# Query rows by three bfloat16 products, routing weights and the last experts' weights loaded in earlier stages

## The chip, the cores and the metric

One core of one Trainium2 chip (trn2). The metric is the device time of the whole program in microseconds; lower is better.

## The reference

A two-layer graph network on 3125 nodes of 256 features and 100,000 edges. Layer 0 is an edge aggregation, a linear attention and an eight-expert layer. Layer 1, on which the change bears, is

```
q, k, v = xn @ Wq + bq, xn @ Wk + bk, xn @ Wv + bv            # 8 heads of 32
scores  = einsum(q[dst], k[src] + ep) * scale * edge_weight    # per edge and head
attn    = segment_softmax(scores, dst)
gnn     = segment_sum(attn * v[src], dst) @ Wo + bo            # then its feed-forward
mix     = linear attention, LayerNorm, relu feed-forward, LayerNorm
x       = xn + gnn + mix
logits  = mean(x) @ Wr + br                                    # one routing for all nodes
top_i, top_w = the two largest of softmax(softmax(logits) * scale)
out     = x + LayerNorm(sum_j top_w[j] * expert[top_i[j]](x) + x)
```

All of it is float32, and the row `q[dst]` of every edge must come out exactly to float32 accuracy, since the softmax follows.

## The kernel before

The program is a row of stages, each a block in which every engine has a queue of its own; a stage ends when all engines are through. Nodes are kept as `NT` = 25 tiles of 128 rows. Edges are sorted by destination and cut into 832 chunks of 128 that each belong to one node tile; 16 chunks make a *window*, and there are `NW` = 52 windows.

`stage_mid` makes q, k and v, spills what later stages need, and runs the linear attention. Its second part works through 14 blocks (`lines`, `NB` = 14) of 128 features by up to 512 nodes: TensorE multiplies (L2372), ScalarE adds the bias (`line`, L2557), VectorE takes the negative part (`below`, L2718), ScalarE exponentiates it (`exp`, L2563), VectorE joins the two (`feature`, L2724), TensorE adds the block into a divisor (L2379). Then come the division (L2772, L2774), the products, a LayerNorm and `rows` (L2792, L2794), which leaves the residual row of the mix branch in `sh.work`; ScalarE's `keep_back` and SyncE's stores of `xt_d` (L2293) end the stage.

`stage_flash` is the edge attention, with the mix branch's feed-forward laid in between. Key and value rows are gathered by GpSimd (`gather`, L2989) into a ring of two windows. The body of one window asks for the rows of window s and closes window a = s - 1. For each quarter g of a window (4 chunks) ScalarE makes a one-hot matrix `mem_t` (`place`, L3126 and L3129), TensorE multiplies it by the q rows of the node tile (`ask`, L3021: 4 products of 128 x 128 by 128 x 256) into the single PSUM tile `query`, and VectorE multiplies the gathered keys by it (`mult`, L3226). Since there is one `query`, `ask(g + 1)` waits for `mult(g)`, and `mult` waits for `ask`. VectorE's order in a body is hand-written: `add(0)`, `within`, `across`, `add(1)`, `lower`, `mult(0)`, `rescale`, `weigh(0)`, `weigh(1)`, `mult(1)`, `add(2)`, `weigh(2)`, two `reduce`, `mult(2)`, `weigh(3)`, `add(3)`, `reduce(2)`, `mult(3)`, `reduce(3)`, `scale`. TensorE's is: transpose of the scores, `up` of the feed-forward (L3058), ends (L3065), `ask(0)`, carried (L3071), `down` (L3077), two small products (L3082, L3083), `ask(1)`, `collect` (L3034) and `fold` (L3041) 0 to 2, `ask(2)`, fold 3, collects 4 and 5, fold 4, `ask(3)`, the rest. A tile whose number is read at run time costs a register instruction ahead of its first product (ISA in the rows of the order).

The q product is float32 and shows as two records (a weight load and a matmul each) per product of the program. SyncE's queue in this stage is, per window: goal (L2948), eight edge loads (L2954), eight flag loads (L2960), steps; and per two windows one tile of the feed-forward's input. VectorE adds the feed-forward's result to `sh.work` in place (L3331). At the end of the stage SyncE waits for the last window but one, loads `xn` back (L2976), and GpSimd adds a bias to it (L3002).

`stage_route` loads the three routing arrays (L3580 to L3582), forms the logits (L3589) and writes the two expert numbers (L3642). `stage_ffx` reads the numbers on SyncE ahead of each of its loads (L2041 to L2043), waits for all three arrays of expert 0 and runs up (L2064) and down (L2073) of both experts, output last.

## Time and profile before

| what | us |
|---|---|
| median of 3 runs (3642.55 to 3644.26) | 3642.98 |
| the profiled execution, its own time | 3640.97 |
| its span, first to last instruction | 3639.0 |
| TensorE busy | 3021.7 |
| VectorE busy | 2119.2 |
| ScalarE busy | 1716.8 |
| GpSimd busy | 1923.4 |

The stages follow each other in the span: edges and aggregation to about 1210, the first experts to about 1550, `stage_mid` to 1853, `stage_flash` from there to 3188, its output projection and feed-forward to 3430, routing to 3443, the last experts to the end. Instruction times are in ns where the rows say so, all others in us; "idle before" is the time for which the engine had nothing to do just before an instruction, with what released it.

### The profile page before, as it was taken

The numbers are of one execution on the slowest core, as the hardware profiler recorded it, in microseconds if no ns is written. First come the engines' busy times: TensorE is split into PE (matmuls) and PEld (weight loads), VectorE is DVE, ScalarE is ACT, GpSimd is POOL, SyncE is SP. The second block draws the span as 40 slices with busy tenths as digits, with TensorE's granted clock in tenths as the row PEclk, the third lists the DMA queues.
The fourth block names the chain that finished last, engine by engine and source line by source line (L and its number), as shares of the span: only waits on it lengthen the run. The fifth ranks groups of instructions, "written<-read, shape, count | busy, mean of one in ns | idle before, by whom it ended". The sixth has DMA issues, their size and how long they took to land. (4 is left out here: it accounts for less than half of the span.)

```text
span 3639.0 us, 50484 instructions
## 1 busy us (share of the span) xinstructions
PE 3021.7 (83%) x12620; PEld 2281.7 (63%) x12620; DVE 2119.2 (58%) x4741; ACT 1716.8 (47%) x3980; POOL 1923.4 (53%) x1876
## 2 busy tenths in 40 slices
PE   2778677778778599779849999999999999889798
PEld 2556555555555588656437777777777777656565
DVE  6333334333334500175559999999999999843415
ACT  2434333333333322233246666667666666542323
POOL 3777777777773344301036666666666666530010
PEclk9777767887868599989769999999999999889899
DMA  6555555555551256641057777777777777510001
GB/s 162 147 146 149 140 156 140 156 141 147 143 146 34 68 197 219 185 160 59 9 182 221 219 215 223 210 219 221 218 216 222 218 214 224 154 67 0 27 0 36
DMA packets 354070, 547.21 MB, mean 150 GB/s; under 512 B 172814, under 2 KB 224275, under 8 KB 353509
## 3 DMA queue, kind: packets, MB, share of 16 engines
q0 software_dynamic: 113216, 348.74, 33.1%
q1 hardware_dynamic: 232710, 183.43, 17.0%
q10 hardware_dynamic: 7887, 12.08, 1.0%
q8 instruction: 104, 1.70, 0.2%
q14 instruction: 153, 1.25, 0.1%
HBM read 493.34 MB, written 51.90 MB: 150 GB/s over the span
## 5 line engine op out<-in xcount | busy, mean ns | idle before, releaser
L2989 POOL DMA_INDIRECT store<-kv_d,src_of x832 | 869.5, 1045 | 422.5 <-issue 245.7
L859 POOL DMA_INDIRECT agg_rows<-xn_d,src_of x832 | 791.5, 951 | 268.4 <-issue 243.1
L1031 PE MATMUL agg_sums<-agg_rows,agg_member 128*128 128x257 f32 x1664 | 582.8, 497 | 255.2 <-DVE acc L923 132.8
L872 ACT ACTIVATE agg_rows<-agg_rows,weight_of 128x256 f32<-128x256 f32 x832 | 375.2, 500 | 614.6 <-DMA agg_rows<-xn_d,src_of 611.7
L1031 PEld LDWEIGHTS agg_sums<-agg_rows,agg_member 128*128 128x128 f32 x1664 | 374.4, 245 | 415.2 <-DVE acc L923 185.2
L923 DVE TENSOR_TENSOR acc<-acc,agg_sums 128x257 f32 x416 | 176.3, 424 | 580.6 <-PE agg_sums L1031 566.1
L3021 PE MATMUL flash_query<-q,flash_mem_t 128*128 x1664 | 412.7, 392 | 50.6 <-DVE store L3226 38.8
L3034 PE MATMUL flash_sums<-store,flash_member 128*128 128x264 f32 x1664 | 424.8, 388 | 2.2 <-DVE store L3291 2.2
L3021 PEld LDWEIGHTS flash_query<-q,flash_mem_t 128*128 128x128 f32 x1664 | 312.7, 193 | 103.7 <-issue 57.4
L3034 PEld LDWEIGHTS flash_sums<-store,flash_member 128*128 128x128 f32 x1664 | 318.4, 191 | 56.8 <-issue 2.2
L3144 ACT ACTIVATE acc<-flash_sums 128x264 f32 x416 | 159.2, 383 | 254.5 <-PE flash_sums L3041 254.5
L3226 DVE TENSOR_TENSOR store<-store,flash_query 128x1024 f32<-128x1024 f32 x208 | 252.3, 1213 | 39.8 <-PE flash_query L3021 39.7
L3041 PE MATMUL flash_sums<-acc,ident 128*128 x832 | 269.5, 406 | 1.9 <-ACT acc L3144 1.5
L3135 ACT ACTIVATE flash_member<-lane,lane_of 128x128 f32<-128x128 f32 x832 | 264.1, 395 | 0.0
L3219 DVE TENSOR_TENSOR store<-store,flash_ep 128x1024 f32<-128x1024 f32 x208 | 252.5, 1215 | 14.8 <-DMA flash_ep<-ep_d 13.5
L3291 DVE TENSOR_TENSOR store<-store,flash_pa 128x1056 f32<-128x1056 f32 x208 | 258.4, 1264 | 0.0
L3230 DVE TENSOR_REDUCE flash_dots<-store 128x32 f32<-128x1024 f32 x208 | 247.8, 1212 | 1.8
L3041 PEld LDWEIGHTS flash_sums<-acc,ident 128*128 128x128 f32 x832 | 145.9, 190 | 64.2 <-issue 48.3
L914 DVE TENSOR_SCALAR agg_member<-lane,lane_of 128x128 f32<-128x128 f32 x832 | 178.9, 304 | 9.5 <-issue 0.4
L1021 PEld LDWEIGHTS agg_edge<-agg_we,agg_feats 128*128 128x128 f32 x832 | 146.8, 249 | 31.4 <-issue 10.5
L1815 DVE TENSOR_TENSOR moe_y<-moe_down,moe_b 128x512 f32<-128x512 f32 x32 | 22.1, 691 | 244.1 <-PE moe_down L1653 244.1
L3126 ACT ACTIVATE flash_mem_t<-flash_goal,minus_row 128x512 f32<-128x512 bf16 x208 | 148.0, 712 | 22.0 <-PE flash_query L3021 15.3
(483 smaller groups left out, 4597.6 us busy)
## 6 DMA issues: line engine op xcount, KB each, us to landing
moe_w<-in_L_ffn_W_dram SPq DMA_DIRECT2D x64, 512.0 KB, 4.5
agg_feats<-in_ef_t_dram SPq DMA_DIRECT2D x208, 128.0 KB
flash_goal<-goal_d SPq DMA_DIRECT2D x52, 512.0 KB, 4.3
agg_rows<-xn_d,src_of POOLq DMA_INDIRECT x832, 2.8
ep_d<-agg_ep SPq DMA_DIRECT2D x52, 256.0 KB
store<-kv_d,src_of POOLq DMA_INDIRECT x832, 4.1
flash_ep<-ep_d SPq DMA_DIRECT2D x416, 32.0 KB
flash_flags<-flags_d SPq DMA_DIRECT2D x416, 32.0 KB
```

Source lines behind the costliest of these rows:

```text
L859: pool.indirect_dma_start(rows[:, q, 0:D], None, sh.xn_d, bass.IndirectOffsetOnAxis(ap=sh.src_of[:, c:c + 1], axis=0)).then_inc(gathered[u ...
L872: act.activation(rows[:, q, 0:D], rows[:, q, 0:D], ACT.Copy, scale=sh.weight_of[:, bass.ds((UI * i + u) * SUBS + k, 1)]).then_inc(weighted, 1)
L1031: last = pe.matmul(sums[:, j % 4, 0:W], member[:, c % (2 * BI * SUBS), :], rows[:, c % NB, :], start=(c % SUBS == 0), stop=(c % SUBS == SU ...
L2989: pool.indirect_dma_start(ring[:, s, :], None, sh.kv_d, bass.IndirectOffsetOnAxis(ap=sh.src_of[:, c:c + 1], axis=0)).then_inc(gathered[p][ ...
L3021: last = pe.matmul(query[:, c * D:(c + 1) * D], mem_t[:, g % 2, c * P:(c + 1) * P], sh.q[:, bass.ds(t, 1), :], start=True, stop=True)
L3034: pe.matmul(sums[:, n % 3, 0:W], member[:, g % 2, c, :], ring[:, a.side * WS + 4 * g + c, HI_], start=(k == 0), stop=False)
L3041: pe.matmul(sums[:, n % 3, 0:W], sh.ident[:, :], sh.acc[:, bass.ds(tiles[n], 1), :, :].rearrange("p a h v -> p (a h v)"), start=False, sto ...
L3135: act.activation(member[:, g % 2, k, :], sh.lane[:, :], ACT.Abs, scale=-1.0, bias=sh.lane_of[:, bass.ds(WS * a.at + (4 * g + k), 1)])
L3219: dve.tensor_tensor(r, r, ep[:, s.side, 4 * g:4 * g + 4, :].unsqueeze(2).to_broadcast([P, 4, H, DH]), ALU.add).then_inc(add_done, 1)
L3226: dve.tensor_tensor(r, r, query[:, :].rearrange("p (k f) -> p k f", k=4), ALU.mult).then_inc(mult_done, 1)
L3230: dve.tensor_reduce(dots[:, g * 4 * H:(g + 1) * 4 * H].rearrange("p (k h) -> p k h", h=H), key_rows(s, g).rearrange("p k (h d) -> p k h d" ...
L3291: dve.tensor_tensor(r, r, e.unsqueeze(3).to_broadcast([P, 4, H, VW]), ALU.mult).then_inc(pv_ready, 1)
```

## The change

The q rows are split exactly into three bfloat16 parts: the upper half of each float32 word (read in place, every second bfloat16 of `sh.q`), the rounded rest, and what is left (`sh.q_low`, in the memory of `stage_mid`'s qkv weights). High and middle part overwrite `sh.q`. `ask` makes three bfloat16 products per chunk where it made one float32 product, all into the same PSUM columns; `mem_t` is bfloat16. The splitting is added to `stage_mid`'s second part: `rest` and `lowest` on VectorE, `parts` on ScalarE, seven pieces of up to four tiles.

To make room, `sh.work` goes to DRAM: five stores in `stage_mid`, one load and one store of a tile per two windows in `stage_flash`, the whole back at its end. Its memory holds the feed-forward's second weights, hidden rows and input. The routing arrays are loaded in the output projection's stage. The last experts' weights are loaded from within `stage_route`, as soon as the expert numbers are written; `stage_ffx` waits for the first weights and bias (32), and for the second weights apart.

```diff
@@ stage_mid, SyncE
+                    sp.wait_ge(rows_done, e)
+                    sp.dma_start(sh.work_d[:, a:e, :], sh.work[:, a:e, :]).then_inc(sh.work_out[n], 16)
@@ stage_mid, ScalarE
+                def parts(n):
+                    a, e = SPLIT[n]
+                    act.wait_ge(rest_ready, n + 1)
+                    act.activation(sh.q_parts[:, a:e, 0:D], sh.q_parts[:, a:e, 1::2], ACT.Copy).then_inc(high_kept, 1)
+                    act.wait_ge(high_kept, n + 1)
+                    act.activation(sh.q_parts[:, a:e, D:2 * D], rest_of(n), ACT.Copy).then_inc(middle_kept, 1)
                     line(q)
                     if q >= 1:
                         exp(q - 1)
+                    if 7 <= q < 7 + len(SPLIT):
+                        parts(q - 7)
@@ stage_mid, VectorE
+                def rest(n):
+                    dve.tensor_tensor(rest_of(n), sh.q[:, a:e, :], sh.q_parts[:, a:e, 1::2], ALU.subtract
+                                      ).then_inc(rest_ready, 1)
+                def lowest(n):
+                    dve.wait_ge(middle_kept, n + 1)
+                    dve.tensor_tensor(sh.q_low[:, a:e, :], rest_of(n), sh.q_parts[:, a:e, D:2 * D], ALU.subtract
+                                      ).then_inc(low_kept, 1)
                 for q in range(6, 10):
                     below(q)
                     feature(q - 1)
+                    rest(q - 6)
+                    if q >= 7:
+                        lowest(q - 7)
@@ stage_flash, SyncE
+                for n in range(used):
+                    sp.wait_ge(sh.work_out[n], 16)
+                def work_load(i):
+                    if i >= 3:
+                        sp.wait_ge(work_stored[i % 3], 16 * (i // 3))
+                    sp.dma_start(work[:, i % 3, :], sh.work_d[:, i, :]).then_inc(work_in[i % 3], 16)
+                def work_store(i):
+                    sp.wait_ge(down_added, i + 2)
+                    sp.dma_start(sh.work_d[:, i, :], work[:, i % 3, :]).then_inc(work_stored[i % 3], 16)
                     sp.wait_ge(up_ready, 2 * i)
                     sp.dma_start(xt_s, ...).then_inc(xt_in, 16)
+                    if i >= 2:
+                        work_store(i - 2)
+                    if i + 1 < NT:
+                        work_load(i + 1)
+                work_store(NT - 2)
+                work_store(NT - 1)
+                for q in range(3):
+                    sp.wait_ge(work_stored[q], 16 * len(range(q, NT, 3)))
+                sp.dma_start(sh.work[:, :, :], sh.work_d).then_inc(sh.work_back, 16)
@@ stage_flash, TensorE, ask
-                            last = pe.matmul(query[:, c * D:(c + 1) * D], mem_t[:, g % 2, c * P:(c + 1) * P],
-                                             sh.q[:, bass.ds(t, 1), :], start=True, stop=True)
+                            to, hot = query[:, c * D:(c + 1) * D], mem_t[:, g % 2, c * P:(c + 1) * P]
+                            pe.matmul(to, hot, sh.q_parts[:, bass.ds(t, 1), 0:D], start=True, stop=False)
+                            pe.matmul(to, hot, sh.q_parts[:, bass.ds(t, 1), D:2 * D], start=False, stop=False)
+                            last = pe.matmul(to, hot, sh.q_low[:, bass.ds(t, 1), :], start=False, stop=True)
@@ stage_flash, VectorE
+                        dve.wait_ge(work_in[i % 3], 16 * (i // 3 + 1))
@@ stage_route, SyncE
+                sp.wait_ge(expert_ready, 1)
+                e = [sp.value_load(sh.expert[0:1, q:q + 1], min_val=0, max_val=7) for q in range(2)]
+                for q in range(2):
+                    for to, of in up_of(q, e[q]):
+                        sp.dma_start(to, of).then_inc(sh.ffx_up_in[q], 16)
+                    sp.dma_start(*down_of(q, e[q])).then_inc(sh.ffx_down_in[q], 16)
@@ stage_ffx, TensorE
-                    pe.wait_ge(weights_in[q], 48)
+                    pe.wait_ge(sh.ffx_up_in[q], 32)
+                        if g == 0:
+                            pe.wait_ge(sh.ffx_down_in[q], 16)
```

TensorE's queue in the body of a window, from the ends to the products after `ask(0)`, before:

```order
L3065 MATMUL flash_small<-flash_z,flash_row_head 8x32
L3021 ISA
L3021 MATMUL flash_query<-q,flash_mem_t 128x256 x2
L3021 ISA
L3021 MATMUL flash_query<-q,flash_mem_t 128x256 x2
L3071 MATMUL flash_small<-flash_carry,flash_head_row 128x32
```

and the first half of the same `ask` now (early is the memory of the low part):

```order
L3091 ISA
L3091 MATMUL flash_query<-q,flash_mem_t 128x256
L3092 ISA
L3092 MATMUL flash_query<-q,flash_mem_t 128x256
L3093 ISA
L3093 MATMUL flash_query<-early,flash_mem_t 128x256
L3091 MATMUL flash_query<-q,flash_mem_t 128x256
L3092 MATMUL flash_query<-q,flash_mem_t 128x256
L3093 MATMUL flash_query<-early,flash_mem_t 128x256
```

Four products (eight records) with two register instructions became twelve products with six.

VectorE's queue in `stage_mid` for blocks 7 and 8, before:

```order
L2718 TENSOR_SCALAR store<-acc 128x512
L2724 SCALAR_TENSOR_TENSOR acc<-acc,store 128x512
```

and now, per block (L2786 is `rest`, L2792 is `lowest`):

```order
L2736 TENSOR_SCALAR store<-acc 128x512
L2742 SCALAR_TENSOR_TENSOR acc<-acc,store 128x512
L2786 TENSOR_TENSOR mid_nr<-q 128x1024
L2792 TENSOR_TENSOR early<-mid_nr,q 128x1024
```

Seven `rest` and seven `lowest`, six of each 128 x 1024 and one 128 x 256, stand between the blocks from 6 to 13.

SyncE's queue in `stage_route`, now (all of it but the branches):

```order
L3654 TENSOR_LOAD expert
L3654 ISA x2
L3654 TENSOR_LOAD expert
L3654 ISA x2
L3657 ISA
L3657 DMA ffx_w<-in_L_ffn_W_dram 128x2x512
L3657 ISA
L3657 DMA ffx_b<-in_L_ffn_b_f_dram 128x4
L3658 DMA ffx_w<-in_L_ffn_W_dram 128x4x256
```

The reads of the expert numbers went from six, one ahead of each load, to two ahead of all, and the bias stands ahead of the second weights.

## Rows read from the trace of the kernel before

**Rows 1.** The page: engine, busy us, share of the span, instructions.
```profile
PE 3021.7 (83%) x12620; PEld 2281.7 (63%) x12620; DVE 2119.2 (58%) x4741; ACT 1716.8 (47%) x3980; POOL 1923.4 (53%) x1876
```
**Rows 2.** Groups of instructions, window 2100 to 3100: busy us, mean ns, idle before.
```profile
L2989 POOL DMA_INDIRECT store<-kv_d,src_of x644 | 675.0, 1048 | 325.1 <-issue 189.2 <-PE flash_sums L3041 136.0
```
**Rows 3.** Waits in 2100 to 3100: us in total, times, longest.
```profile
DVE store L3226 <- PE flash_query L3021: 25.9, 41, 1.6
...
DVE flash_run L3256 <- PE flash_small L3065: 12.8, 40, 0.3
```
**Rows 4.** Waits in the whole span: us in total, times, longest.
```profile
DVE store L3226 <- PE flash_query L3021: 39.7, 55, 4.1
```
**Rows 5.** Timeline of one window, VectorE and then TensorE: start, us, line, idle before.
```profile
2508.82 1.22 DVE L3226 TENSOR_TENSOR store<-store,flash_query 128x1024 f32<-128x1024 f32 x1 [0.61 <-PE flash_query L3021]
...
2499.97 1.99 PE L3021 MATMUL flash_query<-q,flash_mem_t 128*128 x8 [0.68 <-DVE store L3226]
...
2506.82 1.89 PE L3021 MATMUL flash_query<-q,flash_mem_t 128*128 x8
2508.55 0.61 PE L3041 MATMUL flash_sums<-acc,ident 128*128 x2
...
2516.61 1.95 PE L3058 MATMUL flash_up<-flash_xt,store 128*128 128x128 f32 x16
```
**Rows 6.** Timeline of TensorE in the first experts' stage: bfloat16 products at half clock.
```profile
1254.00 1.25 PE L1666 MATMUL moe_turned<-moe_digits,moe_is_low 128*128 128x128 bf16 x10 [1.94 <-ACT moe_digits L1709]
```
**Rows 7.** Instructions of line 3021: duration in ns, least, median, most.
```profile
L3021 PEldq FUSED_REGOPS  x416: 46/46/51, 1871.1 to 3156.2; - x139
```
**Rows 8.** Stretches: us, busy of PE, PEld, DVE, ACT, POOL, granted clock, DMA share, GB/s.
```profile
500.00:600.00 100.00, 71.13 (x240) 51.50 (x240) 35.64 (x121) 38.66 (x90) 75.93 (x80) 0.75 0.56 153
...
1400.00:1500.00 100.00, 92.48 (x446) 79.13 (x447) 8.80 (x13) 27.92 (x62) 49.73 (x51) 1.00 0.68 214
...
2100.00:2300.00 200.00, 190.19 (x906) 153.03 (x905) 186.23 (x289) 137.87 (x333) 135.74 (x130) 1.00 0.75 219
```
**Rows 9.** SyncE's queue, what it waited for in 2100 to 3100.
```profile
SPq L2953 <- DVE store L3226: 237.6, 40, 6.0
SPq L2948 <- ACT flash_mem_t L3126: 193.4, 40, 7.0
```
**Rows 10.** Timeline of `stage_mid`'s blocks: VectorE, then ScalarE.
```profile
1756.61 0.68 DVE L2772 TENSOR_SCALAR store<-mid_zsum 64x512 f32<-64x512 f32 x1 [3.60 <-PE mid_zsum L2379]
...
1739.18 0.69 ACT L2557 ACTIVATE acc<-mid_out,mid_mix_b 128x512 f32<-128x512 f32 x1 [1.71 <-PE mid_out L2372]
```
**Rows 11.** Groups over the span: prices for the added elementwise instructions.
```profile
L1996 DVE TENSOR_TENSOR store<-store,work 128x1024 f32<-128x1024 f32 x6 | 7.4, 1226 | 0.6
...
L2563 ACT ACTIVATE store<-store 128x512 f32<-128x512 f32 x12 | 7.4, 620 | 0.0
...
L890 ACT ACTIVATE agg_mix_kt<-agg_mix_kt,agg_mix_low 128x3125 f32<-128x3125 f32 x1 | 2.9, 2901 | 2.4 <-DVE agg_mix_low L965 2.4
```
**Rows 12.** Timeline of the end of `stage_flash`.
```profile
3172.64 15.45 POOL L3002 TENSOR_TENSOR store<-store 128x1280 f32<-128x1280 f32 x5 [25.67 <-DMA store<-xn_d]
```
**Rows 13.** Timeline of routing and of the last experts' start.
```profile
3431.03 0.17 DVE L3608 TENSOR_SCALAR route_mean<-route_mean 128x2 f32<-128x2 f32 x1
...
3433.83 1.02 PE L3589 MATMUL route_bank<-route_wr,route_mean 128*128 128x8 f32 x4 [4.47 <-DMA route_b<-in_L_ffn_b_dram]
...
3439.82 0.17 DVE L3642 CAST expert<-route_place 128x2 int32<-128x2 uint32 x1
...
3443.91 1.23 DVE L2133 TENSOR_TENSOR store<-store,b_row 128x1024 f32<-128x1024 f32 x1 [0.30 <-PEq L3577]
3444.76 0.40 SPq L2041 DMA_DIRECT2D ffx_w<-in_L_ffn_W_dram  x1
...
3447.09 0.35 SPq L2043 DMA_DIRECT2D ffx_b<-in_L_ffn_b_f_dram  x1
...
3450.60 9.67 PE L2064 MATMUL ffx_up<-store,ffx_w 128*128 128x512 f32 x16 [7.45 <-DMA ffx_b<-in_L_ffn_b_f_dram]
```

More of the change, by code:

```diff
@@ L2000, in _, with stage_ffx @@
                 finish(NGR - 1)
-def stage_ffx(nc, sh, w1_of, w2_of, b1_of, gamma, beta, out):
+def stage_ffx(nc, sh, gamma, beta, out):
     with ExitStack() as ctx:
@@ L2024, in stage_ffx @@
         down = ctx.enter_context(nc.psum_tensor("ffx_down", [P, GT, 512], F32))
-        weights_in = [sem(f"weights_in{q}") for q in range(2)]
         affine_in = sem("affine_in")
@@ L2039, in _ @@
             def _(sp):
-                for q in range(2):
-                    sp.dma_start(w1[:, q], w1_of(q)).then_inc(weights_in[q], 16)
-                    sp.dma_start(w2[:, q], w2_of(q)).then_inc(weights_in[q], 16)
-                    sp.dma_start(b1[:, q], b1_of(q)).then_inc(weights_in[q], 16)
                 for n, v in enumerate((gamma, beta)):
@@ L2172, in stage_mid @@
     LEAD = 2
+    SPLIT = [(a, min(a + 4, NT)) for a in range(0, NT, 4)]
     with ExitStack() as ctx:
@@ L2289, in _ @@
                     sp.dma_start(sh.xn2_d[:, a:e, :], sh.xn[:, a:e, :]).then_inc(spilled, 16)
-                for a, e in BACK:
+                for n, (a, e) in enumerate(BACK):
                     sp.wait_ge(turn3_kept, e)
@@ L2914, in stage_flash @@
         down_added = sem("down_added")
+        work_in = [sem(f"work_in{q}") for q in range(3)]
+        work_stored = [sem(f"work_stored{q}") for q in range(3)]
         def tile_numbers(eng, w):
@@ L2963, in load @@
                                  ).then_inc(flags_in[p], 16)
+                def work_load(i):
[5 more added lines that the diff above has]
+                    sp.dma_start(sh.work_d[:, i, :], work[:, i % 3, :]).then_inc(work_stored[i % 3], 16)
                 load(0, 0, True)
                 load(1, 1, True)
-                sp.dma_start(xt_s[:, :, :], sh.xt_d[0]).then_inc(xt_in, 16)
+                sp.dma_start(xt_s, sh.xt_d[0]).then_inc(xt_in, 16)
+                for n in range(used, len(BACK)):
+                    sp.wait_ge(sh.work_out[n], 16)
+                for i in range(2):
+                    work_load(i)
                 for i in range(1, NT):
@@ L3401, in _ @@
                 sp.dma_start(*gain_load).then_inc(sh.gain_in, 16)
+                for to, of in route_loads:
+                    sp.dma_start(to, of).then_inc(sh.route_in, 16)
             @block.tensor
@@ L3569, in stage_route @@
         bank = ctx.enter_context(nc.psum_tensor("route_bank", [P, 2, 512], F32))
-        loaded = sem("loaded")
+        loaded = sh.route_in
+        expert_ready = sem("expert_ready")
         mean_ready = sem("mean_ready")
@@ L3608, in _ @@
                 dve.tensor_scalar(mean[:, :], mean[:, :], 1.0 / N, None, ALU.mult).then_inc(mean_ready, 1)
+                dve.wait_ge(loaded, 48)
                 dve.wait_ge(prod, 1)
@@ L3641, in _ @@
                 dve.drain()
-                dve.tensor_copy(sh.expert[:, :], place[:, 0:2])
+                dve.tensor_copy(sh.expert[:, :], place[:, 0:2]).then_inc(expert_ready, 1)
                 dve.tensor_copy(place_f[:, :], place[:, 0:2])
@@ L3730, in build @@
         sh.xn_back = ctx.enter_context(nc.semaphore("xn_back"))
+        sh.route_in = ctx.enter_context(nc.semaphore("route_in"))
         sh.bias_in = ctx.enter_context(nc.semaphore("ao_bias_in"))
         sh.xn_stored = ctx.enter_context(nc.semaphore("xn_stored"))
+        sh.work_out = [ctx.enter_context(nc.semaphore(f"work_out{n}")) for n in range(len(BACK))]
+        sh.work_back = ctx.enter_context(nc.semaphore("work_back"))
         with nc.sbuf_tensor("ends", [1, 2, NCH], I32) as sh.ends:
@@ L3802, in build, with up_of, down_of @@
         sh.b2_row = sb("b2_row", [P, D])
-        stage_route(nc, sh, blocks(a["L1_ffn_Wr"]), a["L1_ffn_br"], a["L1_ffn_b2"])
-        def expert1(array, pattern):
-            def part(q):
-                e = nc.sync.value_load(sh.expert[0:1, q:q + 1], min_val=0, max_val=7)
-                return a[array][bass.ds(e, 1)].rearrange(pattern, p=P)
-            return part
-        stage_ffx(nc, sh, expert1("L1_ffn_W1", "e (k p) f -> p (e k) f"), expert1("L1_ffn_W2", "e (k p) f -> p (e k) f"),
-                  expert1("L1_ffn_b1_f", "e p k -> p (e k)"), a["L1_ffn_gamma"], a["L1_ffn_beta"], out)
+        sh.ffx_w1 = sb("ffx_w1", [P, 2, KB, F1])
+        sh.ffx_w2 = sb("ffx_w2", [P, 2, FB, D])
+        sh.ffx_b1 = sb("ffx_b1", [P, 2, FB])
+        sh.ffx_up_in = [ctx.enter_context(nc.semaphore(f"ffx_up_in{q}")) for q in range(2)]
+        sh.ffx_down_in = [ctx.enter_context(nc.semaphore(f"ffx_down_in{q}")) for q in range(2)]
+        def up_of(q, e):
+            return [(sh.ffx_w1[:, q], a["L1_ffn_W1"][bass.ds(e, 1)].rearrange("e (k p) f -> p (e k) f", p=P)),
+                    (sh.ffx_b1[:, q], a["L1_ffn_b1_f"][bass.ds(e, 1)].rearrange("e p k -> p (e k)", p=P))]
+        def down_of(q, e):
+            return sh.ffx_w2[:, q], a["L1_ffn_W2"][bass.ds(e, 1)].rearrange("e (k p) f -> p (e k) f", p=P)
+        stage_route(nc, sh, up_of, down_of)
+        stage_ffx(nc, sh, a["L1_ffn_gamma"], a["L1_ffn_beta"], out)
 def kernel(**inputs):
```

76 lines of the change are left out of this document (52 added, 24 removed).

## The prediction

> **What bounds the kernel now.** The page comes first: TensorE is busy for 83% of the span, VectorE for 58% [rows 1], but these shares are means over stages, so each edit is priced in its own stage. By the stretches, the edge attention (1853 to 3188, over a third of the span) has both engines near their limit: in 200 us TensorE is busy for 190 and VectorE for 186, at the full granted clock of 2.4 GHz [rows 8]. The reader is to see that neither is plainly the bound. The waits tell: in 1000 us VectorE stands 25.9 us for the query product, 41 times, once in each window, thus 0.63 us each, and 12.8 us for the ends product [rows 3]. The timeline shows which: `mult(2)` at 2508.82 waited 0.61 us, and TensorE had started the stretch behind it, `ask(1)` up to `ask(2)`, at 2499.97, as soon as `mult(0)` released it [rows 5]. So TensorE's stretch from `ask(1)` to `ask(2)` is the longer side of a loop by 0.63 us per window, and everywhere else VectorE sets the pace. GpSimd has slack: it waited 136.0 us for TensorE in the same 1000 us [rows 2].
>
> **The q product.** Now `ask(2)` begins at 2506.82 and the fold behind it at 2508.55: 1.73 us for four float32 products, eight records [rows 5]. The change puts twelve bfloat16 products in its place. Per record that is 0.216 us, 512 column passes at 2.4 GHz (0.213): two passes over 256 columns. A bfloat16 product is one record, and two rows bound its pace. Ten bfloat16 products of 128 columns in the first experts' stage take 1.25 us at half clock, at most 0.125 us each with the weight load between them, where one pass per column is 128 / 1.2 GHz = 0.107 [rows 6]. And the feed-forward's 16 pairs of weight load and matmul, which are 256 passes each (two over 128 columns), take 1.95 us at full clock, at most 0.122 each [rows 5]. A bfloat16 product of 256 columns at full clock is 256 passes too: 0.107 us, with the small overheads of these rows 0.11. Twelve are 1.3 us, and an `ask` is 0.4 us shorter. Two of them lie in the stretch: 0.8 us, more than the 0.63 that VectorE waits. So the wait goes, VectorE becomes the only bound, and a window gains 0.63 and not the 1.6 us that TensorE saves. Fifty steady windows give 31.5 us. All waits of this kind in the span are 39.7 us [rows 4]; of the 8 us outside the steady part, at the stage's ends with TensorE partly at half clock, I take 3.5. **Term: -35 us**, between 0 (pace 0.144 or worse, where twelve take the 1.73 of before) and -39.7.
>
> What is late next is the ends product (12.8 us in 1000, a round trip that no edit shortens) [rows 3]. ScalarE's one-hot instructions keep their sizes. Gathers start on TensorE's sums, which come no later, and GpSimd's slack of 136 us covers a window that is 2.6% shorter [rows 2].
>
> **SyncE's queue in the attention.** Added per two windows are a store and a load of 128 KB, and the load waits for the store issued just ahead of it, so SyncE stands for a transfer's landing, some 4 us, with the next goal load behind. In 1000 us the queue waits 237.6 + 193.4 = 431 us, 10.8 per window, because its loads are issued two windows ahead [rows 9]. I cost it at nothing; if the cover were gone it would be 4 us in each of 24 pairs, 96 us. VectorE's new wait (for the row loaded two windows before) costs nothing for the same reason.
>
> **The split in `stage_mid`.** A 128 x 1024 VectorE operation takes 1.23 us [rows 11]; twelve of them and two quarter pieces are 15.3 us. A ScalarE copy of 1024 is not shown: between 620 ns for 512 and 2901 for 3125 [rows 11] the line gives 1.07 us; with the two quarter pieces 13.5 us. Per block ScalarE now idles 1.71 us [rows 10] between its two instructions; `parts` needs 2 x 1.07 plus a wait for its own first copy, say 0.2, so a block of 2.9 us becomes 3.5 to 3.7. That is 0.7 us for each of five full blocks and nearly the whole 2.3 us for the two of 53 columns, 8 us, of which TensorE's tail of divisor products, on which VectorE now waits 3.60 us [rows 10], takes back about 3. **Term: +5 us**, between 0 (all in idle time) and +15.3 (VectorE's work in a row).
>
> **The handover.** Five work stores share the queue with `xt_d`, the last beside the first loads of the attention. No row prices it; the nearest, the small routing load that holds TensorE from 3431.03 to 3433.83 [rows 13], says that one landing is 2.8 us. **Term: +1 us**, between 0 and 2.8. The reload of `sh.work` runs beside the last window; the stage's end is set by GpSimd's bias (15.45 us behind the `xn` load, 3172.64 to 3188.1) [rows 12], which moves with the windows. Nothing.
>
> **Routing and last experts.** The mean is ready at 3431.2 and the logits start at 3433.83, held by the load [rows 13]: 2.6 us go. The expert number is written at 3440.0, then at 3437.4. Before, SyncE had its first load out 0.85 us after the stage began (3443.91 to 3444.76) with one number read; two reads put the first load at 3439.1, the bias 0.4 later. The bias landed 3.5 us after its issue (3447.09 to 3450.60), behind 1 MB of weights [rows 13]; now only half stands ahead of it. TensorE starts at about 3443.3, against 3450.60: **term -7 us**, between -5.7 (the whole 5.84 us from first load to start stays) and -9.2 (start with the stage, at 3441.4). TensorE then runs to the end, so it counts in full.
>
> **Sum.** -35 + 5 + 1 - 7 = -36 us. The profiled execution took 3640.97 us around a span of 3639.0, so 3605; the median of the runs shown stands 2.0 above it: **3607 us**.
>
> **Rivals.** *(1) Not faster in the loop.* An `ask` has six register instructions of 46 ns where it had two [rows 7], and `ask(1)` starts cold behind a wait, when the sequencer cannot have run ahead. If these show between products, twelve take 1.3 + 0.25 = 1.55 us, a window gains 0.36 instead of 0.63, the loop 19 instead of 35: 3623. With TensorE less busy the granted clock could also fall: it was 0.75 where TensorE was busy 71%, but 1.00 at 92% [rows 8], and here it goes from 95% to about 89%. At a mean of 0.93 its saving of 1.6 us in 24.7 is all given back, which leaves -1 us: 3642, and this is also the case where the change does not do what it says.
>
> *(2) Slower.* The weight load shows. If a load of 128 columns does not hide behind the product ahead, a bfloat16 product costs 0.11 + 0.11 = 0.22 us, an `ask` 2.6 us, and TensorE's work per window, 23.5 us now, grows by 3.6 to 27.1 against a window of 24.7: +2.4 us in 52 windows, +125 us, so 3767. It decides from 0.144 us per product on. Against it are both rows of pace: pairs of a load and a 256-pass matmul at 0.122 us or less [rows 5], and bfloat16 pairs at half clock at 0.125 or less, where a load and a matmul in a row would be two times 0.107 [rows 6].
>
> The Trainium skill has a rule for this rival: "TensorE: Matmul & The Clock Gate", Part 3, on what overlaps, says that a weight load overlaps a running matmul only where the two use different row groups, which none here do. By that rule the sum would be that of this rival, some 3770; the trace disagrees with it: 0.122 us at most for a full-size pair.
>
> *(3) SyncE is late.* Its stalls come in 24 of 52 windows; the case needs a landing of over 10 us. A part of it would give 3620 to 3650.
>
> **How the numbers follow.** Forecast, 3597 to 3618: 0.66. Part of the gain, 3618 to 3635: 0.15. Gain lost, 3635 to 3650: 0.11. Slower: 0.08. A measurement of this kernel tells 0.2% (7.3 us) from no change. Faster by more, below 3635.7, is 0.82; within it 0.08; slower, part of the third case and all of the fourth, 0.10. The range of 3595 to 3633 holds the first case and most of the second, 8 in 10.
>
> **What would show it.** Right: VectorE's wait for the query product near zero in the steady part; windows of 24.05 us; an `ask` of 12 records in 1.3 to 1.5 us; granted clock 1.00; `stage_mid`'s blocks 3.5 us or more; TensorE's first `up` of the last experts 7 us closer to the routing's start. Wrong: spacing of 0.144 us or more; VectorE waits for gathers or rows; a clock under 1.00; SyncE's stores landing late with ScalarE waiting for the goal.

## The result and the profile after

The changed kernel took 3612.4 us (median of 4 runs, 3607.2 to 3618.2), the kernel before 3643.6 beside it (4 runs, 3642.6 to 3648.8): 0.9912 of the time, 95% interval 0.9891 to 0.9932. That is 31 us less, where 36 were forecast, and inside the range. The profiled execution of the changed kernel is its longest, 3618.2 us around a span of 3616.4, so a later execution of the same kernel (c1_after, span 3608.6) stands beside it below.

A gain of this kind (35 us) was measured once more, on one of the three chips of the experiments (which of them the result ran on, if any, isn't known). On the two others both kernels are 18 to 22% slower, and the change makes the kernel 2.5 to 2.7% **slower**. The experiments tell of that too.

The page of the changed kernel, engines (busy us, share, instructions), against [rows 1]: TensorE has 76 us less work and is still the busiest by far over the whole span.

```profile
PE 2945.9 (81%) x13452; PEld 2189.2 (61%) x13452; DVE 2129.9 (59%) x4755; ACT 1721.1 (48%) x3994; POOL 1964.5 (54%) x1876
```

In the edge attention the order has turned. From 2100 to 3100 us, before and then now (us, busy of PE, PEld, DVE, ACT, POOL, granted clock, DMA share, GB/s), TensorE was ahead of VectorE by 24 us and is now 26 us behind it:

```profile
2100.00:3100.00 1000.00, 951.95 (x4518) 767.02 (x4517) 927.75 (x1430) 688.23 (x1655) 674.98 (x644) 1.00 0.75 218
```

```profile
2100.00:3100.00 1000.00, 921.22 (x5288) 718.86 (x5286) 946.73 (x1475) 696.69 (x1692) 721.13 (x662) 0.99 0.80 228
```

The waits of VectorE and SyncE's queue from 2100 to 3100 us of the changed kernel (us in total, times, longest), against [rows 3, 9]:

```profile
DVE flash_run L3327 <- PE flash_small L3136: 13.4, 42, 0.3
DVE store L3297 <- PE flash_query L3093: 4.3, 4, 1.4
DVE store L3290 <- DMA store<-kv_d,src_of: 3.1, 6, 0.7
...
SPq L3000 <- DVE store L3297: 222.2, 41, 5.6
SPq L2995 <- ACT flash_mem_t L3197: 113.8, 27, 6.9
SPq L3015 <- DMA work_d<-work: 59.7, 19, 4.8
```

The wait for the query product fell from 25.9 us in 41 windows to 4.3 in 4 waits. The ends product is what it was. SyncE does stand for its own stores now, 3.1 us each, and still idles 9.6 us per window in all (397 us in 41 windows). GpSimd stays behind: it waited 84.0 us for TensorE where it had 136.0 [rows 2].

```profile
L3058 POOL DMA_INDIRECT store<-kv_d,src_of x662 | 722.1, 1091 | 279.2 <-issue 195.2 <-PE flash_sums L3112 84.0
```

One `ask` on the timeline (start, us, line), from its first product to the fold behind it:

```profile
2912.10 0.27 PE L3091 MATMUL flash_query<-q,flash_mem_t 128*128 x1
2912.21 0.27 PE L3092 MATMUL flash_query<-q,flash_mem_t 128*128 x1
2912.32 0.27 PE L3093 MATMUL flash_query<-early,flash_mem_t 128*128 x1
2912.43 0.27 PE L3091 MATMUL flash_query<-q,flash_mem_t 128*128 x1
...
2913.41 0.61 PE L3112 MATMUL flash_sums<-acc,ident 128*128 x2
```

Twelve products in 1.31 us, 0.109 each, with a weight load of 128 columns between any two; the estimate was 0.11 and 1.3. `ask(1)`, which starts behind a wait, takes longer: 1.54 us to the next product in this window (2905.45 to 2906.99), 1.49 in the median of 41, where it took 1.82 before.

Where the time went, by the first or last start of the same instruction in each profiled execution (us, differences to the kernel before in brackets; the only trace of the kernel before is that of the result). Times of single instructions are from their own lines of the trace.

| from, to | before | after | c1_after |
|---|---|---|---|
| start to the last statistics of `stage_mid`'s first part | 1666.8 | 1671.1 (+4.3) | 1670.1 (+3.3) |
| to the bias row behind the divisors (split beside the blocks) | 93.8 | 95.1 (+1.3) | 95.1 (+1.3) |
| to the last row of `work` | 85.9 | 88.5 (+2.6) | 88.5 (+2.6) |
| to the first product of keys and query rows (handover) | 31.5 | 33.0 (+1.5) | 32.5 (+1.0) |
| to the last of them (52 windows) | 1281.3 | 1255.7 (-25.6) | 1249.6 (-31.7) |
| to the end of the span | 479.7 | 473.0 (-6.7) | 472.8 (-6.9) |
| span | 3639.0 | 3616.4 (-22.6) | 3608.6 (-30.4) |

The first row holds almost only code that the change doesn't touch; it differs by as much between executions (1668.0 in b1_no_traffic and 1673.0 in b4_both, the same code up to there). The handover varies too, from 32.5 in c1_after to 36.1 in b1_no_traffic with the same code in that stretch, and 33.8 in a1r_f32_query.

**The loop.** Window ends (the `scaled` instruction) of the changed kernel from 2100 to 3120: 41 periods in 993.2 us, 24.22 each. Before, the same instruction starts at 2142.4 and, 39 windows on, at 3109.0: 24.79. The gain in a steady window is 0.57 us.

```profile
L3307 DVE SCALAR_TENSOR_TENSOR flash_scaled<-flash_dots,weight_of x42: 372/373/377, 2122.9 to 3116.1; 128x128 f32<-128x128 f32 x42
```

What is left of the query wait comes with falls of the granted clock. VectorE's row, then three stretches (us, busy of PE, PEld, DVE, ACT, POOL, granted clock, DMA share, GB/s):

```profile
2939.77 1.22 DVE L3297 TENSOR_TENSOR store<-store,flash_query 128x1024 f32<-128x1024 f32 x1 [1.36 <-PE flash_query L3093]
...
2925.00:2931.00 6.00, 4.36 (x27) 3.19 (x26) 5.08 (x12) 2.81 (x9) 4.77 (x5) 1.00 0.78 203
2931.00:2934.00 3.00, 3.00 (x13) 2.22 (x11) 3.00 (x4) 0.72 (x1) 2.32 (x2) 0.57 0.87 257
2934.00:2940.00 6.00, 6.00 (x33) 4.98 (x32) 4.64 (x5) 5.11 (x12) 2.47 (x3) 0.93 0.42 121
```

After a stretch with TensorE busy for 4.36 of 6 us the clock is at 0.57, almost all of it at the level of 1.2 GHz, for some 3 us; the sums behind `ask(1)` take longer and `ask(2)` is 1.4 us late. From 2100 to 3100 us the clock falls three times, at 2132.7, 2398.9 and 2931.4, and a long wait stands some 9 us behind each (1.41, 1.32 and 1.36 us, at 2141.6, 2408.2 and 2939.8). In c1_after it is the same: falls at 2128.3, 2370.7 and 2732.5, waits of 1.41, 1.45 and 1.21 us at 2137.5, 2379.0 and 2741.8. The kernel before had one such fall in this stretch, at 2325.9. At full clock waits of 0.17 to 0.23 us are left, three in either trace. In a window without a fall the last product of `ask(2)` starts at 2913.30 and lasts 0.27 us, and VectorE takes its rows at 2913.68: TensorE's stretch is now about as long as VectorE's, not far shorter.

**The end.** Routing and the last experts of the changed kernel, against [rows 13]:

```profile
3415.47 0.17 DVE L3684 TENSOR_SCALAR route_mean<-route_mean 128x2 f32<-128x2 f32 x1
3415.78 0.99 PE L3665 MATMUL route_bank<-route_wr,route_mean 128*128 128x8 f32 x4 [1.99 <-DVE route_mean L3684]
...
3422.18 0.17 DVE L3719 CAST expert<-route_place 128x2 int32<-128x2 uint32 x1
...
3423.86 0.40 SPq L3657 DMA_DIRECT2D ffx_w<-in_L_ffn_W_dram  x1
3424.45 0.36 SPq L3657 DMA_DIRECT2D ffx_b<-in_L_ffn_b_f_dram  x1
...
3428.01 2.93 PE L2058 MATMUL ffx_up<-store,ffx_w 128*128 128x512 f32 x3 [2.50 <-DMA ffx_b<-in_L_ffn_b_f_dram]
```

The logits wait for nothing (0.31 us behind the mean, before 2.80), and from the mean to TensorE's first product of the last experts are 12.5 us where there were 19.6. It still waits for the small bias, which lands 3.6 us after its issue.

**`stage_mid`.** The copies of the split share ScalarE with the blocks. The `line` of two blocks in a row, and then VectorE at the division:

```profile
1750.39 0.67 ACT L2565 ACTIVATE acc<-mid_out,mid_mix_b 128x512 f32<-128x512 f32 x1
1753.52 0.67 ACT L2565 ACTIVATE acc<-mid_out,mid_mix_b 128x512 f32<-128x512 f32 x1
...
1762.15 0.68 DVE L2811 TENSOR_SCALAR store<-mid_zsum 64x512 f32<-64x512 f32 x1 [0.41 <-PE mid_zsum L2387]
```

A block takes 3.13 us where it took 2.91 or 2.92, and VectorE waits 0.41 us for TensorE's tail where it waited 3.60 [rows 10].

Something was lost behind the blocks. ScalarE at the first norms of the last part, changed kernel, then the kernel before:

```profile
1792.01 1.28 ACT L2595 ACT_TABLE_LOAD   x1 [30.57 <-DVE mid_var L2630]
1793.30 0.21 ACT L2595 ACTIVATE mid_std<-mid_var 128x6 f32<-128x6 f32 x1
```

```profile
1752.79 1.28 ACT L2577 ACT_TABLE_LOAD   x1
1785.13 0.21 ACT L2577 ACTIVATE mid_std<-mid_var 128x6 f32<-128x6 f32 x1 [31.07 <-DVE mid_var L2612]
```

Before, the activation table was loaded at once and then ScalarE waited 31 us. Now a second wait (`low_kept`) stands ahead of the square root's own, and the table is loaded behind both, in the path: VectorE's reciprocal waited 1.61 us for the square root where it had waited 0.27.

```profile
1793.54 0.19 DVE L2824 RECIPROCAL mid_rstd<-mid_std 128x6 f32<-128x6 f32 x1 [1.61 <-ACT mid_std L2595]
```

### The profile page after: what moved, and what is told of

Its sections match the earlier page's. It is cut to its first block and busy times, and to the rows that moved or that the text cites. A ratio compares the mean times of both kernels' runs of the same rounds, so it can differ in the third digit from the quotient of the medians.

```text
span 3616.4 us, 53081 instructions
## 1 busy us (share of the span) xinstructions
PE 2945.9 (81%) x13452; PEld 2189.2 (61%) x13452; DVE 2129.9 (59%) x4755; ACT 1721.1 (48%) x3994; POOL 1964.5 (54%) x1876
## 3 DMA queue, kind: packets, MB, share of 16 engines
q0 software_dynamic: 113216, 348.74, 33.8%
## 5 line engine op out<-in xcount | busy, mean ns | idle before, releaser
L3058 POOL DMA_INDIRECT store<-kv_d,src_of x832 | 905.4, 1088 | 361.1 <-issue 246.1
L3091 PE MATMUL flash_query<-q,flash_mem_t 128*128 x832 | 232.0, 279 | 54.5 <-DVE store L3297 42.4
L3290 DVE TENSOR_TENSOR store<-store,flash_ep 128x1024 f32<-128x1024 f32 x208 | 253.1, 1217 | 22.6 <-DMA flash_ep<-ep_d 14.4
L3093 PE MATMUL flash_query<-early,flash_mem_t 128*128 x832 | 232.6, 280 | 0.0
L3092 PE MATMUL flash_query<-q,flash_mem_t 128*128 x832 | 232.4, 279 | 0.0
L3112 PEld LDWEIGHTS flash_sums<-acc,ident 128*128 128x128 f32 x832 | 138.5, 191 | 59.2 <-issue 46.9
L3197 ACT ACTIVATE flash_mem_t<-flash_goal,minus_row 128x512 bf16<-128x512 bf16 x208 | 148.0, 712 | 21.8 <-PE flash_query L3093 14.9
```

What stands on the lines that cost most here:

```text
L3058: pool.indirect_dma_start(ring[:, s, :], None, sh.kv_d, bass.IndirectOffsetOnAxis(ap=sh.src_of[:, c:c + 1], axis=0)).then_inc(gathered[p][ ...
L3093: last = pe.matmul(to, hot, sh.q_low[:, bass.ds(t, 1), :], start=False, stop=True)
L3112: pe.matmul(sums[:, n % 3, 0:W], sh.ident[:, :], sh.acc[:, bass.ds(tiles[n], 1), :, :].rearrange("p a h v -> p (a h v)"), start=False, sto ...
L3290: dve.tensor_tensor(r, r, ep[:, s.side, 4 * g:4 * g + 4, :].unsqueeze(2).to_broadcast([P, 4, H, DH]), ALU.add).then_inc(add_done, 1)
```

## The experiments

Theory A was: VectorE alone sets a window now, SyncE's traffic is free. Its rival B: the gain is smaller than forecast because TensorE (or SyncE's traffic) still sets part of it. The first four runs (c0, a1, a3, a4) fell on a chip on which the stages with gathers are slower, the next four (c1, a1r, b1, b4) on one like that of the result, the last four (c2, a3r, a4r, b5) again on a slow one. Ratios are to the kernel before on the same chip.

**c0_after, c1_after, c2_after**: the changed kernel, unedited.

> The changed kernel itself, once more, as the measure for the three runs beside it. Its four runs so far lay between 3607.2 and 3618.2 us; if the spread is its own, the median of more runs is 3608 to 3616. Theory A (VectorE sets the loop, TensorE has no more part in it): 24.2 us per window again, and VectorE's wait for the query product 1.3 to 1.4 us long and only in windows in which the granted clock falls below 1.00 for a few us. Theory B (the rest of the missing gain is TensorE's): the wait also in windows with the clock at 1.00 throughout.

> The changed kernel once more, beside another run of the kernel before. In the runs of c0_after both kernels were 18 and 22% slower than in the result (4296 and 4410 us), already in the aggregation, which the change doesn't touch: there the signals of TensorE reached the other engines only when the gathers' transfers had ended, all at once, after pauses of 5 to 10 us. If that belongs to one chip or one time, this run gives 3607 to 3618 us and 0.991 of the kernel before; if it belongs to the kernel, some 4400 us again.

> The changed kernel, as the measure for the three runs beside it. Without the pauses of TensorE's signals: 3607 to 3613 us, loop (first to last product of keys and query rows) 1249 to 1256 us. With them: some 4400 us.

| | before | changed | ratio, 95% interval |
|---|---|---|---|
| c0_after (first chip) | 4296.1 | 4410.2 | 1.0265, 1.0241 to 1.0289 |
| c1_after (second) | 3645.0 | 3609.8 | 0.9902, 0.9886 to 0.9919 |
| c2_after (third) | 4305.0 | 4418.2 | 1.0252, 1.0227 to 1.0277 |

The times go with the chip; as each chip was used at one time only, the two can't be told apart for certain. On the slow chips only the stages with gathers are longer. In c0_after the last 473.0 us, from the last product of keys and query rows to the end, are those of the result's chip (473.0), and so are the 95.1 us of the blocks; but the aggregation, which the change doesn't touch, ends at 1379.3 instead of 1124.1, and the 52 windows take 1796.2 instead of 1255.7. VectorE's waits in the loop of c0_after, first to last (the profile calls a releaser that it can't place "remote"):

```profile
DVE flash_run L3327 <- remote: 445.9, 44, 10.8
```

One such pause on the timeline of c0_after:

```profile
2726.20 0.23 PE L3136 MATMUL flash_small<-flash_z,flash_row_head 128*8 128x32 f32 x2 [0.59 <-issue]
...
2733.44 0.95 POOL L3058 DMA_INDIRECT store<-kv_d,src_of  x1 [0.30 <-issue]
2736.47 1.14 ACT L3230 ACTIVATE work<-flash_up,flash_b 128x128 f32<-128x128 f32 x4 [11.34 <-DMA xn_d<-store]
2736.52 0.23 DVE L3327 TENSOR_TENSOR_SCAN flash_run<-flash_steps,flash_run,flash_small 8x16 f32<-8x16 f32 x1 [10.37 <-remote]
```

TensorE starts the ends product at 2726.20, and VectorE, which needs nothing else, goes on at 2736.52. ScalarE resumes at the same moment from an `up` product that TensorE had started at 2723.66. TensorE still runs `ask(0)`, whose last product starts at 2727.65; from there to the end of the pause TensorE, VectorE and ScalarE do nothing, GpSimd issues the last gather of its window at 2733.44, and the DMA engines are busy to the end of the pause (last two columns but one: clock, DMA share):

```profile
2732.00:2736.00 4.00, 0.00 (x0) 0.00 (x0) 0.00 (x0) 0.00 (x0) 1.89 (x2) 0.50 0.78 212
2736.00:2740.00 4.00, 2.46 (x7) 2.04 (x8) 3.07 (x13) 3.02 (x9) 0.00 (x0) 0.50 0.22 67
```

The trace has the time of the semaphore events too, and they settle which side is late. The ends product is over at 2726.43, and its event is recorded at 2736.49; that of `up` (over at 2725.62) is recorded at 2736.45, and that of `ask(0)` (over at 2727.92) at 2736.62. In 42 of the loop's 52 windows of c0_after, and in 41 of c2_after, the ends product's event stands more than 7 us behind the product's end, mostly 10.0 to 10.5, and VectorE starts 0.02 to 0.03 us behind the event. In c1_after it stands 0.01 us behind the product in every window. So on these chips TensorE's signals reach the others late, all at once, about when the gathers have run out. Whether another engine's signal would be held as well isn't shown: in the pause above none is due, and on the slow chips many events of VectorE are missing from the trace. Beside it SyncE's issue of eight edge-product loads, which reads their addresses from memory, is stretched: 8 us long on the chip of the result, 16.75 here, and it begins 3.2 us ahead of the ends product. The changed kernel, then c0_after:

```profile
2704.10 8.46 SPq L3001 DMA_DIRECT2D flash_ep<-ep_d  x8
```

```profile
2722.97 16.75 SPq L3001 DMA_DIRECT2D flash_ep<-ep_d  x8
```

What holds the signals isn't shown; the profile has no row for it. The Trainium skill ("DMA: Bandwidth & Descriptors", Latency and other measured facts) names, as its own best guess, contention at the ports of the rings that hold the descriptors of GpSimd's gathers, for slower DMA engines; no run here tests whether that is the cause.

**a1_f32_query, a1r_f32_query**: the float32 query product again, without the split; the traffic of `work` and the prefetches stay. The one-hot matrix is float32 in the memory where the split's lowest part was.

```diff
-                            pe.matmul(to, hot, sh.q_parts[:, bass.ds(t, 1), 0:D], start=True, stop=False)
-                            pe.matmul(to, hot, sh.q_parts[:, bass.ds(t, 1), D:2 * D], start=False, stop=False)
-                            last = pe.matmul(to, hot, sh.q_low[:, bass.ds(t, 1), :], start=False, stop=True)
+                            last = pe.matmul(to, hot, sh.q[:, bass.ds(t, 1), :], start=True, stop=True)
```

> The changed kernel with the query rows by one float32 one-hot product as before, and with the exact split of q left out of stage_mid (it is not needed then); the one-hot matrix is float32 again. The traffic of `work` and the prefetches stay. The query product's part of the gain is the difference to the changed kernel, that of the prefetches and the traffic the difference to the kernel before. By the trace: the loop goes back to 24.7 to 24.8 us per window, the last-experts part stays at -9.7 us (2.6 routing, 7.1 last experts), stage_mid loses 3.8 us of additions. If SyncE's traffic of `work` costs nothing: 3643.6 - 9.7 = 3634 us (3632 to 3636). If it costs something in the loop (gathers later, 0.05 us per window and up to 4.5 us at the end): 3636 to 3641.

> The same as a1_f32_query (float32 query product, no split; traffic of `work` and prefetches kept), to have it without the pauses. Without pauses: 24.7 to 24.8 us per window; in all 3634 us (3632 to 3636) if SyncE's traffic of `work` costs nothing, 3636 to 3641 if it costs something in the loop. With the pauses: 0.998 of the kernel before, as measured, some 120 us below the changed kernel.

On the chip of c1_after: 3639.0 us, 0.9982 (0.9972 to 0.9992), 29 us above the changed kernel, so the product with its split is 29 of the 35 us gained on this chip. Its loop takes 1281.1 us against 1249.6, 31.5 more, and the wait is back (its waits in the loop, then those of c1_after):

```profile
DVE store L3286 <- PE flash_query L3082: 37.8, 54, 4.2
DVE flash_run L3316 <- PE flash_small L3125: 17.4, 51, 1.5
...
DVE store L3279 <- DMA store<-kv_d,src_of: 4.6, 3, 2.6
```

```profile
DVE store L3297 <- PE flash_query L3093: 8.5, 7, 3.1
DVE store L3290 <- DMA store<-kv_d,src_of: 5.1, 3, 4.2
```

The 29.3 us less of query wait are most of the 31.5. Against the kernel before it gains 6 us where 9.7 were expected: against the trace of the kernel before the end is 7.6 us shorter, the handover 2.3 longer (33.8 for 31.5), and 3.3 lie ahead of all edits.

On the slow chip the same kernel is 0.9983 of the kernel before, and the changed one 1.0265: there the query products with their split, and not the traffic or the prefetches, cost 121 us. The loop is 107.6 of them (1688.6 against 1796.2); 8.9 lie ahead of all edits. VectorE's pauses of that kind, a1_f32_query:

```profile
DVE flash_ahead L3306 <- remote: 177.9, 33, 5.8
DVE flash_run L3316 <- remote: 61.2, 8, 11.0
```

They are some 5 us at the start of a window, where the changed kernel has 10 us a few instructions on. TensorE's clock, with the loop's longer idle, is 0.84 in the changed kernel and 0.88 here. Why the pause finds the faster program at a worse place isn't settled.

**a3_two, a3r_two** (8 products per ask; the third product, so the lowest part of each query row, is left out) and **a4_four, a4r_four** (16, the lowest part twice):

```diff
-                            last = pe.matmul(to, hot, sh.q_low[:, bass.ds(t, 1), :], start=False, stop=True)
+                            pe.matmul(to, hot, sh.q_low[:, bass.ds(t, 1), :], start=False, stop=False)
+                            last = pe.matmul(to, hot, sh.q_low[:, bass.ds(t, 1), :], start=False, stop=True)
```

> The changed kernel with the third (lowest) product of each query row left out: 8 in place of 12 bfloat16 products per ask, some 0.44 us less for each of four asks in a window; all else, the split too, stays. Theory A (VectorE alone sets the window): the remaining query wait of 4.3 us per 41 windows is all there is to win, so 0 to -5 us against the changed kernel, window 24.1 to 24.2 us. Theory B (TensorE still sets part of the window): -0.44 us in 50 windows or more, 3590 us or less. A third outcome would be a loss: TensorE waits longer and more often, and its clock falls more often.

> As a3_two (8 products per ask, the lowest part left out of the loop), to have it without the pauses. Theory A (VectorE sets the window; only the 1.4 us waits at falls of the clock are left to win): loop 0 to 5 us shorter than the changed kernel's 1250. Theory B (TensorE still sets a part): 20 us or more shorter, below 1230. A loss is possible too, if TensorE waits oftener and its clock falls oftener.

> The changed kernel with the lowest product done twice: 16 in place of 12 bfloat16 products per ask, some 1.76 us per ask, about the 1.73 us of the float32 ask before. The prediction's point from which the change gains nothing in the loop was 0.144 us per product with twelve, which is 1.73 us per ask. If that holds, the loop is back at 24.7 to 24.8 us per window: +25 to +32 us against the changed kernel, 3636 to 3645 us. If the third ask had room behind VectorE's work, less: +10 us or so. By one window of the trace it has some 0.2 us: two asks of +0.44 us less 0.2 make +0.7 us per window, +35 us, 3645 us or a little more.

> As a4_four (16 products per ask), without the pauses. The prediction's point was 0.144 us per product with twelve, an ask of 1.73 us, from which the loop gains nothing. Sixteen at 0.11 are 1.76 us. If the point holds, the loop is back at the 1281 us of before, so +31 us against the changed kernel, total 3636 to 3645. If other instructions of the larger stream cost something on TensorE, more than that.

All four ran on slow chips, so what they were to decide on a chip without pauses stays undecided. Two products per row: 4378.4 and 4388.6, ratios 1.0201 and 1.0184. Three: 4410.2 and 4418.2. Four: 4347.6 and 4357.2, ratios 1.0106 and 1.0115. Both chips agree within 10 us, and neither theory's number is near: twelve products are slower than eight and than sixteen. In the loop a4_four is 69 us faster than c0_after (1727.2 against 1796.2) with 0.44 us more work in each ask. So more work on TensorE makes this loop shorter there. The pauses lie at another place and are shorter in sum: VectorE's waits on "remote" are 331 us in a4_four's loop and 512 in c0_after's. That this is the cause is argued and not tested. VectorE's rows of a4_four,

```profile
DVE store L3298 <- remote: 174.6, 47, 12.2
DVE flash_run L3328 <- remote: 78.8, 20, 7.2
```

The sixteen products take 0.11 us each here too (first to last start 1.65 us), and the clock is 0.89 (0.84). Whether the forecast's point of 0.144 us per product is where the gain ends was not measured on a chip without pauses.

**b1_no_traffic**: three tiles of `work` are loaded and kept, all other loads and stores in the loop are gone.

```diff
-                    if i >= 2:
-                        work_store(i - 2)
-                    if i + 1 < NT:
+                    if i + 1 < 3:
                         work_load(i + 1)
```

> The changed kernel without the traffic of `work` in the loop: three tiles are loaded at the start and never stored or reloaded, so 24 loads and 25 stores of 128 KB and SyncE's waits for them are gone, and `work` comes back without the feed-forward's sums (this part of the computation is left out). Theory A (that traffic is free): within 2 us of the changed kernel. Theory B (it makes the gathers late): VectorE's waits for gathers (3.1 us in 41 windows, 4.5 us before the last) go, -4 to -8 us. With the pauses of the signals I expect no more than -10 us: they end with the gathers, not with this traffic.

3611.9 us beside the changed kernel's 3609.8, the loop 1249.1 against 1249.6. The waits for gathers don't go:

```profile
DVE store L3285 <- DMA store<-kv_d,src_of: 7.0, 4, 5.9
```

So theory A holds: the traffic costs nothing, and the gathers' new lateness (8.1 us in the loop of the result's execution, 1.1 before) is not its doing. Its cause stays open; GpSimd's slack has shrunk, and from 2100 to 3100 us a gather takes 4.9 us from issue to landing (median; 4.4 in c1_after) where it took 4.1 before.

**b4_both**: `work` loaded in its own step, and `low_kept` awaited behind the square root.

```diff
-                for i in range(2):
-                    work_load(i)
+                work_load(0)
...
-                    if i + 1 < NT:
-                        work_load(i + 1)
+                    work_load(i)
...
-                act.wait_ge(low_kept, len(SPLIT))
...
                     act.wait_ge(less3_ready, g + 1)
+                    if g == 0:
+                        act.wait_ge(low_kept, len(SPLIT))
```

> The changed kernel with two waits moved. SyncE loads tile i of `work` in step i and not a step ahead, so it no longer stands 3 us at the store of two steps before (59.7 us in 19 waits of the steady part); and ScalarE's wait for the lowest part of the split stands behind the square root of the last norms, so the activation table of 1.28 us is loaded in ScalarE's idle 30 us again and not in the path of stage_mid. The second is worth -1.3 us by the trace; the first 0 if SyncE's wait hid, and up to -4.5 us if it was what made the gathers or the goal late. So -1 to -6 us against the changed kernel.

```profile
1763.41 1.28 ACT L2594 ACT_TABLE_LOAD   x1
1792.38 0.21 ACT L2594 ACTIVATE mid_std<-mid_var 128x6 f32<-128x6 f32 x1 [27.69 <-DVE mid_var L2631]
```

The table is loaded in the idle time again and VectorE waits 0.27 us. The part of `stage_mid` from the bias row to the last row of `work` took 82.1 us, 6.4 less than in c1_after, of which the table explains 1.3. The rest goes with the level of TensorE's clock there: from the divisors to the last row of `work` it is at the lower level for 44.6 us, and for 57.8 in c1_after. That part varies by 3 us with no edit at all (85.6 in c2_after, with 51.5 us at the lower level, against 88.5). But the whole took 3610.3 us against 3609.8: the handover was 2.5 us longer (35.0), and the part ahead of it 3. A gain of 1.3 us is below what these runs tell. The loop (1248.9) doesn't feel SyncE's shorter stand, as with b1_no_traffic.

**b5_first_load**: the table's edit, and the first two windows' loads issued ahead of the feed-forward's weights at the start of `stage_flash` (eight lines moved behind `load(1, 1, True)`).

> The changed kernel with two edits: ScalarE's wait for the lowest part behind the square root (the activation table of 1.28 us off stage_mid's path, as in b4_both, where this part of stage_mid was 6.4 us shorter), and at the start of stage_flash SyncE issues the loads of the first two windows before the feed-forward's weights, which now stand some 3.5 us ahead of them while VectorE waits 14 us for the first edge products. stage_mid -1.3 us by the table alone, up to -6.4 if the clock follows as in b4_both; the stage's start -3.5 us if the first loads' time to land stays, 0 if the first gathers are what is slow. So -3 to -10 us against the changed kernel.

It fell on a slow chip: 4419.5 us against 4418.2. The handover was 26.4 us against 34.9, so the first loads do land earlier; but the first window then ended at 2169.2 as in c2_after (2169.0), so all of it was lost again within that window. The loop as a whole was 26.7 us longer in the profiled execution, which was the slowest of the five (4434.0 us). Whether it is faster on the other chips was not tried.

## Why the prediction was right

The time lies in the range, 5 us above the forecast. Its bound and its mechanism hold, for chips without the pauses; of its sizes the split's is off, and the handover's may be luck.

- *The q product.* The pace of 0.11 us and the ask of 1.3 are what was measured (0.109, 1.31). If the register instructions of the first rival cost anything, it is in `ask(1)`, behind its wait: 1.49 us in the median instead of 1.31; but before it was longer too, 1.82 instead of 1.73. VectorE has become the bound by the traces (its waits for the product at full clock are 0.23 us or less); the runs that were to test it, with 8 and 16 products, fell on slow chips. The term of -35 was too large: -31.7 in c1_after, -25.6 in the result's profiled execution. The window of before is 24.79 and not 24.7, and of the wait of 0.63 us 0.1 stays, with short falls of the clock; so it is 24.15 to 24.22 and not 24.05. The rest are mostly waits for gathers, 5.1 and 8.1 us where there was 1.1, 4.2 and 4.5 of them at once. "Gathers start on TensorE's sums, which come no later" missed them. The clock's rival was right as a mechanism and far too large in size: three falls in 41 windows.
- *The split.* "+5" was mis-sized: 1.3 us up to the divisors. TensorE's tail took back 3.2 us (VectorE waits 0.41 and not 3.60), as forecast. What was too large are the 8 us for the blocks, some 4.5 by this reckoning: a block is 3.13 us and not 3.5 to 3.7, since the two copies take 2.04 us from the first one's start to the next `line`, and not 2.34: the second starts 0.04 us behind the first one's end and not 0.2, and the next `line` starts before its end. So the sign "blocks 3.5 us or more" did not come. But 2.6 us came behind it that no term had. 1.3 are the table load: the working counted the added instructions and their waits in the blocks, but not the wait added behind them, which the table load came to stand behind. The other 1.3 are TensorE's products behind the divisors, longer at the lower level of the clock.
- *SyncE.* "I cost it at nothing" holds: taking the traffic away gains nothing. Its stand was 3.1 us each and not 4, and SyncE had 9.6 us to spare per window.
- *Handover* +1.0 to +1.5, forecast +1; since it varies by 3.6 us with the same code, that it came so close is luck. *Routing and last experts* -6.7 to -6.9 to the end, forecast -7, by the two steps named: the load of the logits and the earlier weights.
- The remaining 3 to 4 us lie ahead of all edits. Executions of the same code differ by 5 us there; but the one trace of the kernel before is the shortest of all (1666.8), so a small part that belongs to the changed kernel isn't excluded.

By terms in c1_after: 3.3 + 1.3 + 2.6 + 1.0 - 31.7 - 6.9 = -30.4 us; the first of the prediction's cases, 3597 to 3618, is the one that came.

What it did not foresee at all is the other kind of chip. There the sign is that of the rival "slower", with nothing of its mechanism: the product's pace is the same.

## What to carry to other kernels

Where two engines hold a loop between them, a faster one gains only the wait of the other: multiply that wait by the windows, and look then for short falls of the clock and for the next queue. A wait put at the end of a phase on ScalarE can push a table load out of idle time; put it behind the instruction that needs the new table. And measure a change to a tight loop on more than one chip before calling it a gain: here the sign turned.

## What was not expected of the hardware

- Two of the three chips of the experiments run the stages with gathers much slower (the windows 1796 us instead of 1250), with the rest unchanged (473.0 us at the end on both). TensorE's signals come in bursts there: the ends product's event stands 10 us behind the product in most windows, where it is 0.01 us on the other chip, and the pauses end about with the gathers' transfers; SyncE's issue of address-reading loads is stretched from 8.5 to 16.75 us.
- On such a chip more TensorE work can be faster: 16 products per ask 4348 us, 12 products 4410, 8 products 4378.
- TensorE's clock fell to its lower level for some 3 us after six in which TensorE was busy for 4.4, and such a fall costs VectorE 1.2 to 1.45 us (six falls in two traces).
